# Decay sums of a gated delta-rule layer by a VectorE scan over broadcast gates, the state's decays made once and broadcast by DMA

## The reference, cut to what matters

```
dt = softplus(x @ Wa + dt_bias);  g = dt * (-exp(A_log))          # one number per token and head
def step(M, (q_t, k_t, v_t, b_t, g_t)):                            # M is 128 x 128 per sequence and head
    M = M * exp(g_t)
    Mk = einsum('bhd,bhdv->bhv', k_t, M)
    M = M + einsum('bhd,bhv->bhdv', k_t, (v_t - Mk) * b_t)
    o_t = einsum('bhd,bhdv->bhv', q_t, M)
out = out * rsqrt(mean(out*out) + eps) * norm_w * silu(z);  y = out @ Wout
```

## Time and profile before

| what | value |
|---|---|
| time, median of 3 runs | 2031.08 us (2026.42 to 2033.64) |
| span of the profiled execution (it has no other time) | 2031.7 us |
| PE busy | 1915.2 us (94%) |
| DVE, ACT, POOL busy | 1128.8, 934.1, 743.1 us |
| DMA queue of SP | 84.83 MB, 16.4% of 16 engines |
| mean granted TensorE clock | 0.958 |
| chain that ended last | PE 49%, issue 25%, POOL 10%, DVE 7%, ACT 4%, DMA 3% |

### The profile page before, as it was taken

The page is one execution under the profiler, slowest core; times in us unless marked ns, Lnnn a source line. Parts: engine busy times, 40 slices in busy tenths (PEclk is TensorE's granted clock), DMA queues, the critical chain, the costliest instruction groups (busy, mean ns, idle before and its releaser), DMA issues.

```text
span 2031.7 us, 45678 instructions
## 1 busy us (share of the span) xinstructions
PE 1915.2 (94%) x16962; PEld 1561.4 (77%) x16962; DVE 1128.8 (56%) x2048; ACT 934.1 (46%) x2987; POOL 743.1 (37%) x1143
## 2 busy tenths in 40 slices
PE   5899999999999999999999998999997799999999
PEld 3688888888888888888888887888886565656574
DVE  5656565665656575656656665657563442534433
ACT  2455554646464555646464645555563321213121
POOL 1255453636363554536363535445452000000000
PEclk9899998999998999989999999989997899999999
DMA  3011111112010111111120101021114513121110
GB/s 101 16 33 32 33 40 25 34 30 42 22 38 22 38 32 33 39 25 37 28 43 22 38 22 38 23 41 34 31 24 144 146 36 93 42 83 52 55 27 21
DMA packets 220196, 87.10 MB, mean 43 GB/s; under 512 B 138320, under 2 KB 204240, under 8 KB 219280
## 3 DMA queue, kind: packets, MB, share of 16 engines
q1 hardware_dynamic: 220048, 84.83, 16.4%
HBM read 57.28 MB, written 27.53 MB: 42 GB/s over the span
## 4 chain that ended last, share of the span: by engine, by line
PE 49%; issue 25%; POOL 10%; DVE 7%; ACT 4%; DMA 3%; SPq 1%; POOLq 1%; DVEq 0%; ACTq 0%
PE bank L558 17%; PE bank L858 4%; PE bank L808 3%; DVE vT L1406 2%; POOL blkT L1774 2%; PE bank L817 2%; PE bank L770 2%; POOL prod L1770 2%; PE bank L759 2%; PE bank L678 2%; ACT vv L1074 2%; PE bank L802 2%; POOL k_tok L1740 2%; PE bank L824 1%; DMA blkT_d<-blkT 1%
## 5 line engine op out<-in xcount | busy, mean ns | idle before, releaser
L558 PE MATMUL bank<-x_hi,w_hi 128*128 128x512 f32 x1024 | 433.5, 423 | 13.4 <-DVE vT L1406 7.1
L558 PE MATMUL bank<-x_hi,w_lo 128*128 128x512 f32 x1024 | 410.3, 401 | 0.0
L558 PE MATMUL bank<-x_lo,w_hi 128*128 128x512 f32 x1024 | 408.7, 399 | 1.1 <-issue 1.1
L558 PEld LDWEIGHTS bank<-x_hi,w_hi 128*128 128x128 f32 x1024 | 197.9, 193 | 56.1 <-issue 13.9
L558 PEld LDWEIGHTS bank<-x_hi,w_lo 128*128 128x128 f32 x1024 | 196.7, 192 | 43.8
L558 PEld LDWEIGHTS bank<-x_lo,w_hi 128*128 128x128 f32 x1024 | 197.7, 193 | 33.2 <-issue 1.6
L1406 DVE SCALAR_TENSOR_TENSOR qT<-bank,cw,qT 128x511 f32<-128x511 f32 (+2 forms) x192 | 142.1, 747 | 51.1 <-ACT qT L1041 46.5
L1830 POOL TENSOR_TENSOR rstd<-ve,mhalf 128x1 f32<-128x1 f32 x32 | 17.4, 544 | 386.8 <-DVE ve L1588 386.8
L1406 DVE SCALAR_TENSOR_TENSOR kT<-bank,cw,kT 128x511 f32<-128x511 f32 (+2 forms) x192 | 143.3, 747 | 9.9 <-ACT kT L1041 4.9
L1206 ACT ACTIVATE o_tmp<-bank 128x128 f32<-128x128 f32 x256 | 67.4, 278 | 175.5 <-PE bank L824 175.5
L1406 DVE SCALAR_TENSOR_TENSOR vT<-bank,cw,vT 128x511 f32<-128x511 f32 (+2 forms) x192 | 143.2, 746 | 6.8 <-ACT vT L1041 2.3
(11 more groups left out here) (221 smaller groups left out, 4446.2 us busy)
## 6 DMA issues: line engine op xcount, KB each, us to landing
w_raw<-in_w_heads SPq DMA_DIRECT2D x64, 256.0 KB, 2.8
o_d<-og SPq DMA_DIRECT2D x64, 256.0 KB, 2.6
o_raw<-o_d SPq DMA_DIRECT2D x16, 1024.0 KB, 6.2
x_in<-in_x SPq DMA_DIRECT2D x16, 256.0 KB, 3.3
blkN_d<-nT SPq DMA_DIRECT2D x64, 64.0 KB, 2.1
t<-blkT_d SPq DMA_DIRECT2D x64, 64.0 KB, 2.4
wo_raw<-in_w_out SPq DMA_DIRECT2D x4, 1024.0 KB, 9.1
x_res<-in_x SPq DMA_DIRECT2D x16, 256.0 KB, 2.7
```

Source lines behind the costliest of these rows:

```text
L558: last = mm(bank[bk][:, :], w[:, kind % 2, d, :], xx[:, d, b * S:(b + 1) * S], start=(n == 0), stop=(n == 3 * ND - 1))
```

## The change

Before, the decay sums of a chunk were made by two matmuls of 128 x 512 (the gates' high and low part), and the sums for `gam` by two more, from `gt` of POOL, and ACT took the exponential of both. Now:

- Once, ahead of the heads, PE makes rows of all heads' gates and of their sums, ACT copies the one and exponentiates the other, and SP stores both to DRAM (`g_d`, `gam_d`).
- In each head SP loads 2048 numbers of `gam_d` into all 128 partitions (1 MB in SBUF) and the same from `g_d` for the next head.
- DVE turns the gates into decay sums by four scans per head over 512 elements: (previous + gate) times a mask that is 0 or 1. ACT exponentiates them.
- All 16 matmuls of 128 x 512 per head, the eight instructions of `gt` on POOL, two of its three small copies and the four exponentials of `gam` on ACT are gone.

```diff
--- before.py
+++ after.py
@@ sync
+            def load_g(h):
+
+                sp.dma_start(decay[:, :, :, :].rearrange("p c b t -> p (c b t)"),
+                             g_d[h].rearrange("c b t -> (c b t)").unsqueeze(0).to_broadcast([P, UNITS * P])).then_inc(g_in, 16)
+
+            def load_gam(h):
+                sp.dma_start(gam[:, :, :, :].rearrange("p c b t -> p (c b t)"),
+                             gam_d[h].rearrange("c b t -> (c b t)").unsqueeze(0).to_broadcast([P, UNITS * P])).then_inc(gam_in, 16)
+
+            sp.wait_ge(g_rows_done, 2)
+            for rows, dst in ((g_rows, g_d), (gam_rows, gam_d)):
+                sp.dma_start(dst.rearrange("(i h) c b t -> (h c b) i t", i=2), rows[:, :, :]).then_inc(g_out, 16)
+            sp.wait_ge(g_out, 16 * 2)
+            load_g(0)
...
             def head(h, more):
+                sp.wait_ge(sg_done, 2 * h)
+                hold(sp, "sp")
+                sp.wait_ge(kg_done, 3 * h)
+                sp.wait_ge(qg_done, 3 * h)
+                hold(sp, "sp")
+                load_gam(h)
                 sp.wait_ge(nT_done, 4 * h + 4)
...
                 if more:
+                    sp.wait_ge(decay_done, 4 * h + 4)
+                    hold(sp, "sp")
+                    load_g(h + 1)
                     sp.wait_ge(wlo_done, 4 * h + 3)
                     load_weight(h + 1, K_)
@@ tensor
                 if JOB_BANK[job] == 3 and at == 0:
-                    pe.wait_ge(decay_done, 4 * h + 4)
+                    pe.wait_ge(w_done, 4 * h)
...
+            def decay_rows():
+
+                pe.wait_ge(ba_done, B)
+                pe.wait_ge(tokens_ready, 1)
+                for i in range(2):
+                    part = g_all[:, i * H // 2:(i + 1) * H // 2, :].rearrange("p h u -> p (h u)")
+                    mm(bank[2][:, i * P:(i + 1) * P], part, tri[:, :], start=True, stop=True)
+                    last = tr(bank[3][:, i * P:(i + 1) * P], part, ident[:, :])
+                last.then_inc(g_mm, 1)
...
                 for c in range(NC):
-                    pe.wait_ge(gt_done, 4 * h + c + 1)
-                    pe.wait_ge(decay_done, 4 * h + c)
-                    hi, lo = gt[c % 2][:, 0, :, :], gt[c % 2][:, 1, :, :]
-                    mm(bank[3][:, :], after_r[:, :], hi, start=True, stop=False)
-                    mm(bank[3][:, :], after_r[:, :], lo, start=False, stop=True).then_inc(decay_mm, 1)
...
-                    pe.wait_ge(gam_done, 4 * h + c)
-                    mm(bank[gam_bank(c)][:, :], ones_r[:, :], hi, start=True, stop=False)
-                    mm(bank[gam_bank(c)][:, :], ones_r[:, :], lo, start=False, stop=True).then_inc(gam_mm, 1)
-                    if c == 1:
-                        pe.wait_ge(gam_done, 4 * h + 1)
@@ scalar
-                act.wait_ge(kg_done, 3 * h)
-                act.wait_ge(qg_done, 3 * h)
-                act.wait_ge(sg_done, 2 * h)
-                for c in range(NC):
-                    act.wait_ge(decay_mm, 4 * h + c + 1)
-                    fn(pT[:, :, c, :], grid(3), ACT.Exp).then_inc(decay_done, 1)
+                for c in range(NC):
+                    act.wait_ge(scan_done, 4 * h + c + 1)
+                    fn(pT[:, :, c, :], decay[:, c, :, :], ACT.Exp).then_inc(decay_done, 1)
...
-                    act.wait_ge(gam_mm, 4 * h + c + 1)
-                    fn(gam[:, :, c, :], grid(gam_bank(c)), ACT.Exp).then_inc(gam_done, 1)
@@ vector
+            def decays(h):
+                dve.wait_ge(g_in, 16 * h + 16)
+                for c in range(NC):
+                    step_c = decay[:, c, :, :].rearrange("p b t -> p (b t)")
+                    nc.vector.tensor_tensor_scan(step_c, step_c, after[:, :, :].rearrange("p b t -> p (b t)"), 0.0,
+                                                 ALU.add, ALU.mult).then_inc(scan_done, 1)
+
...
             conv(0, V_, 2)
+            decays(0)
             split(0, Q_)
...
+                if more:
+                    decays(h + 1)
                 dve.wait_ge(t32_in, 64 * h + 64)
@@ gpsimd
-                for v, o in ((ghi_h, gt[c % 2][:, 0, :, :]), (glo_h, gt[c % 2][:, 1, :, :])):
-                    last = tt(o, tri[:, :].unsqueeze(1).to_broadcast([P, B, P]), spread(v[:, :, c]), ALU.mult)
-                last.then_inc(gt_done, 1)
...
-                decays(h, 2)
-                scaled(0)
-                decays(h, 3)
-                scaled(1)
-                scaled(2)
-                scaled(3)
+                for c in range(NC):
+                    scaled(c)
...
-                pool.wait_ge(gam_done, 4 * h + 4)
+                pool.wait_ge(gam_in, 16 * h + 16)
```

More of the change, by code:

```diff
@@ L113, in layer @@
     beta_inv = sb("beta_inv", [P, H, B, NC])
-    g_hi = sb("g_hi", [P, H, B, NC], F32R)
-    g_lo = sb("g_lo", [P, H, B, NC], F32R)
+    after = sb("after", [P, B, P])
     beta_inv_h = sb("beta_inv_h", [P, B, NC])
-    ghi_h = sb("ghi_h", [P, B, NC])
-    glo_h = sb("glo_h", [P, B, NC])
     k_sq = sb("k_sq", [P, B, NC])
@@ L145, in layer @@
     nT = sb("nT", [P, B, NC, P])
-    gam = sb("gam", [P, B, NC, P])
-    gt_0 = sb("gt_0", [P, 2, B, P], F32R)
+    gam = sb("gam", [P, NC, B, P])
+    decay = sb("decay", [P, NC, B, P])
+    y32 = sb("y32", [P, NC, B, PAIR])
     y64 = sb("y64", [P, NC, B, P // 2])
-    y1 = sb("y1", [P, 2, B, P])
+    y16 = sb("y16", [P, NC, B, BLK])
     w1 = sb("w1", [P, 2, B, P])
@@ L155, in layer @@
     prod = sb("prod", [P, BLK * BLK // 4])
[L156 to L159, removed]
+    blkN = at(place["y16"][0], "blkN", [P, BLK, BLK])
     blkT = at(place["w1"][0], "blkT", [P, BLK, BLK])
@@ L238, in layer @@
     blkT_d = nc.dram_tensor("blkT_d", [NPAIR, UNITS, PAIR, PAIR], F32, kind="Internal").ap()
+    g_d = nc.dram_tensor("g_d", [H, NC, B, P], F32, kind="Internal").ap()
+    gam_d = nc.dram_tensor("gam_d", [H, NC, B, P], F32, kind="Internal").ap()
     o_d = nc.dram_tensor("o_d", [H, P, B, NC, P], F32, kind="Internal").ap()
@@ L1029, in _, with decay_rows @@
             fn(sp_l[:, :, :], sp_e[:, :, :], ACT.Ln, bias=1.0).then_inc(sp_act, 1)
+            def decay_rows():
+                act.wait_ge(g_mm, 1)
+                fn(gam_rows[:, :, :], bank[2][:, 0:2 * P].rearrange("p (i t) -> p i t", i=2), ACT.Exp).then_inc(g_rows_done, 1)
+                fn(g_rows[:, :, :], bank[3][:, 0:2 * P].rearrange("p (i t) -> p i t", i=2), ACT.Copy).then_inc(g_rows_done, 1)
             def dest(kind, b):
@@ L1689, in _ @@
             triangle(tri[:, :], ALU.is_ge, 0.0, 1.0, -1, 1)
-            triangle(mask[:, :], ALU.is_gt, 0.0, 1.0, 1, -1)
-            chain(nc.gpsimd.tensor_copy(after_r[:, :], mask[:, :]))
-            chain(memset(mask[:, :], 1.0))
-            chain(nc.gpsimd.tensor_copy(ones_r[:, :], mask[:, :]))
+            chain(memset(after[:, :, :], 1.0))
+            chain(nc.gpsimd.affine_select(out=after[:, :, :], in_=after[:, :, :], compare_op=ALU.is_gt, fill=0.0, base=0,
+                                          pattern=[[0, B], [1, P]], channel_multiplier=-1))
             chain(memset(minus_half[:, :], -0.5))
@@ L1786, in head @@
                 for c in range(1, NC):
-                    tt(qT[:, :, c, :], qT[:, :, c, :], gam[:, :, c, :], ALU.mult).then_inc(qg_done, 1)
+                    tt(qT[:, :, c, :], qT[:, :, c, :], gam[:, c, :, :], ALU.mult).then_inc(qg_done, 1)
                 pool.wait_ge(qg_done, 3 * h + 3)
@@ L1802, in head @@
                     pool.wait_ge(o_mm, 4 * h + c)
-                    tt(state[:, (c + 1) % 2, :, :], state[:, c % 2, :, :], spread(gam[:, :, c, P - 1]), ALU.mult).then_inc(sg_done, 1)
+                    tt(state[:, (c + 1) % 2, :, :], state[:, c % 2, :, :], spread(gam[:, c, :, P - 1]), ALU.mult).then_inc(sg_done, 1)
                     deviation(c - 1)
```

41 lines of the change are left out of this document (14 added, 27 removed).

## The result

The changed kernel takes 2123.5 us (median of 4 runs, 2118.2 to 2125.9) against 2032.4 for the kernel before (4 runs, 2026.4 to 2036.7): ratio 1.0447, 95% interval 1.0419 to 1.0474. That is 91 us slower; the forecast was 73 slower, 2105. The profiled execution is the fastest of the four, 2118.2 us, with a span of 2116.5 (84.8 more than before). The ratios of this document compare executions of the usual, faster state alone, which leaves out two of the ten runs of the first experiment.

A forecast was written before the change was run, and what follows sets the result against it. Bound: PE (94% busy) and an equally long chain `nT`, DRAM, POOL, DRAM to the join. Heads 1 to 14 at 5.7 us make 80, +6 first head, +1 last, -14 clock: +73, 2105 us; range 2025 to 2150.

The forecast's parts named there:

- the queue: SP's queue at a head's start: the 1 MB `gam` load ahead of the `nT` stores lengthens the chain by 2.5 us.
- clock gain of 14 us: After the join: longer PE waits raise the mean granted clock from 0.74 to 0.88, 1.7 us in each of 8 heads.
- head 0: First head: 4 us for its own scans, 3 for next head's scans meeting POOL, less 0.9 of chunk loop: +6.
- The lower end of 0: SP's queue: the `gam` load costs the chain 0 us if the small `nT` stores pass it; ruled out by ring order.
- The scans that hold POOL: POOL's substitution: four steps each wait for a DVE scan of 1.23 us, 4 x 1.13 = 4.5 us on the chain.
- The chunk loop: PE's chunk loop without the matmuls: last `k_inv`, `nT`, `og` and V convolution come 0.9 us earlier per head, of 3.7 possible.
- The 8 heads that were to gain: Heads expected to change to the higher mean clock behind the join once PE waits there, 1.7 us each.
- The last head: Last head, without scans for a next one: 2.5 for the load, less 0.4 spare and 0.9 chunk loop, +1.
- Scans that don't hold POOL: Rival at POOL's steps: none or only one of the scans holds POOL; 1.2 us per head, 2045 to 2054; chance 0.16.
- scans of 2.3 us: Rival on DVE: scans take 2.3 us each, the chain 8.8 instead of 4.5; +60, 2165 us; chance 0.07.
- The rival on the other side: Neither load nor scans reach the chain, only the chunk loop's 0.9 us per head is left: 2022 us; chance 0.11.
- PE's saving came through whole: Rival on PE: the removed matmuls' 59 us all come off the time, 1977 us; chance 0.05.

The follow-up runs named there:

- the first experiment: Changed kernel with the `gam` load behind the next head's K and V weights, not ahead of the `nT` stores: 2047.15 us, 1.0037 of the kernel before.
- the best kernel: Changed kernel with both 1 MB loads ahead of the last `og` store and the scans between the Q0 and Q1 convolutions: 2009.74 us, ratio 0.9886.

## Why the prediction was right

The mechanism, its two places and the sign were right; the sum was 12 us below the profiled difference (73 against 85), and several of its terms were off in size. That it came so close is partly luck: the queue was priced 1.6 us too low per head and the scans 1.2 too high, which makes 7.0 us for both where 7.4 were measured. A clock gain of 14 us that didn't come and 9 us too many for head 0 offset each other in part.

- **The queue**, forecast 2.5 us, measured 4.13 per head. The place was right: the load is issued behind `og` and ahead of the stores of `nT`, and moving it away takes it back (POOL starts at 9.95 behind the weights and at 9.71 ahead of `og`). The step that failed in size was "1 MB holds the 16 engines for 2.5 us; its issue, 0.5 us as others, lies inside that". The load went at some 330 GB/s and not at the 416 of the row taken, and the issue did not lie inside: the first store of `nT` is issued 1.0 us later with all and with half of the load, and the line through both sizes leaves 0.7 us fixed. The lower end of 0, small stores that pass the load, is excluded too. The rest, 0.3 us, is a `blkN` read that lands later.
- **The scans that hold POOL**, forecast 4.5 us, measured 3.30. The scan takes 1.24 us (start to start 1.18: 47.2 us for 40), as forecast from twice the elements' time of a plain instruction; the Trainium skill's "DVE: opcode table, instruction layouts, handler registers and perf-mode slots", section on datapath and trigger behaviour, says half throughput, and the trace agrees. Four POOL steps meet four scans, as forecast. But they took 4.55 us, 1.28 for the first and 1.08 to 1.10 for the others, where the forecast added a wait of 1.13 to a step's own 0.3. "Each wait for a scan less the 0.1 us between two of their own" should have been a scan's pitch, 4.72 / 4 = 1.18, less a whole step's pitch of 0.37: 0.8 us each, 3.2 in all.
- **The two depend on each other.** Alone the scans lengthen the way to the join by 2.0 us and the load by 3.5; together it is 6.6. The load pushes POOL's substitution further into the time of the scans. The forecast had this (it placed the scans by the load's delay).
- **The chunk loop**, forecast -0.9, measured -0.94: of 3.7 us of matmuls only that came through, and PE's waits for `k_tok` (11.7 us) and V (13.5) took the rest. Its wait for `o_tmp` (0.5 us per head) was not foreseen. Nor were the 0.64 us per head less from POOL's end to `t32`, whose cause is open.
- **The clock**, forecast -14 us, did not come:

```profile
1108.00:1120.00 12.00, 4.31 (x32) 3.77 (x30) 2.18 (x2) 2.71 (x14) 10.16 (x17) 0.90 0.30 37
1120.00:1135.00 15.00, 14.74 (x475) 12.42 (x476) 10.73 (x20) 7.38 (x19) 3.74 (x3) 0.74 0.05 18
```

The last three numbers of such a row are the granted clock, the DMA share and GB/s. The first stretch is the wait (PE busy for 4.3 of 12 us), the second the join behind it. The forecast took 0.88 for the second from one pair of stretches in the earlier trace rows; here it is 0.74, and the low time from join to chunk loop is 9.5 us per head instead of 6.8. The two stretches of the earlier trace rows lay at different places, 0 to 14 and 9 to 22 us behind their joins, and two heads were too few to read a trend from. The 8 heads that were to gain don't follow from the earlier trace rows either, by which PE waited in 7 of 10. By the pitches above, 2.7 us more of low clock would cost 1.2 us, but this stretch grew by 0.27 only. The traces show why: the low clock moved. The same head before (first two) and after, each from its join on:

```profile
1061.00:1071.00 10.00, 9.52 (x396) 7.84 (x396) 7.51 (x14) 5.46 (x16) 3.20 (x3) 1.00 0.02 5
1071.00:1085.00 14.00, 12.45 (x144) 11.49 (x144) 6.83 (x13) 3.52 (x8) 1.05 (x2) 0.76 0.08 21
1120.00:1130.00 10.00, 9.81 (x305) 8.27 (x307) 6.98 (x12) 3.64 (x11) 0.70 (x1) 0.60 0.07 26
1130.00:1143.00 13.00, 12.88 (x256) 11.58 (x250) 9.42 (x17) 6.36 (x20) 4.60 (x5) 1.00 0.07 23
```

  Over heads 1 to 14, the first 10 us behind the join have 6.3 us of low clock instead of 2.2, as the clock now falls during the wait; the time behind them has 3.2 instead of 4.6, in 5 heads instead of 7. Heads without a late stretch take 47.3 us from join to chunk loop, with 6.6 us of early low clock; before, 46.7 us with 3.9. That is 0.2 us per us. Heads with a late stretch, 9 us long on average, take 4 to 5 us more (52.1, before 50.9), 0.5 us per us. As an estimate from these, 1.5 us less of late low clock gave back 0.7 us per head, and 4.2 us more of early cost 0.9: part of the forecast gain came, and the early low time took it back.
- **The ends.** Head 0 was forecast at +6 and measured at -2.8 (2.5 ahead of its last `nT`, -5.2 behind it, where between join and chunk loop it had 6.8 us at the low clock before, which can cost 3.4, and none after). Ahead of the last `nT`, where 4 were counted for its scans, 2.5 were added. The last head has the load too, as forecast, but it cost 3.4 and what follows 1.9 more, whose cause is open.
- **The rivals.** Scans that don't hold POOL, and scans of 2.3 us, are excluded by the rows of one head. The rival on the other side was this kernel with both costs moved off the chain: it asked for less than 1.3 us of delay per head and gave 2022. The kernel that meets this, with a join at 28.65 us, took 2010. PE's saving came through whole nowhere: with both costs away 29 us of 59 did.

## What to carry to other kernels

Removing work from the busiest engine pays only as far as the path beside it gets shorter too; here the change is worth 1.1%, once nothing is added to the chain, and its 16 matmuls per head cost 1.4% when they are put back. Price an addition by what stands behind it in its queue: the same load of 1 MB per head cost 3 to 4% ahead of four small stores, and nothing where the queue would have waited for another engine. A VectorE instruction with two SBUF inputs belongs where GpSimd waits, not where VectorE happens to be idle.

## What the runs showed of the hardware that was not expected

- A 1 MB load with 8 KB rows delayed small stores queued behind it by 3.8 us, 0.5 MB by 2.25: 0.7 us and 3.1 us per MB. Rows read 128 times from one place or distinct ones made 0.2 us of difference.
- VectorE and GpSimd went step by step: a GpSimd step of 0.29 us became one of 1.08 to 1.28 beside scans, one per scan; the scans lost next to nothing by it (4.72 us for four, and 4.59 in the best kernel, where POOL waits beside them). Beside transposes with one SBUF input it kept its 0.3.
- With matmuls added in one stretch, the time at the low clock in a later stretch, where none was added, rose from 5.6 to 7.6 us per head, by two long stretches in 14 heads. Why is open.
- A microsecond at 1.2 GHz had no single price: within 10 us behind the join's start, where products of 16 x 16 to 32 x 32 stand between the projections, 2.7 us more of it came with 0.6 us more per head; later in the head 9 us came with 4 to 5.
